# A vision tower with windowed mixer, 16-head attention and routed experts: the attention operands stacked by SBUF copies on row halves, with one reduction and one exponential per pair of heads

## What is computed

```python
q = split_heads(holo_linear(x, basis_q, phase_q, amp_q))     # 16 heads of 16
k = split_heads(holo_linear(x, basis_k, phase_k, amp_k))
attn = jnp.einsum('bhqd,bhkd->bhqk', q, k) * scale
attn = jax.nn.softmax(attn, axis=-1)
out = jnp.einsum('bhqk,bhkd->bhqd', attn, v)
```

## Time and profile before

| | |
|---|---|
| median of 3 runs | 2960.3 us (2955.33 to 2965.71) |
| the profiled execution | 2954.87 us, its span 2953.0 us |
| PE busy (matmul) over the span | 2595.7 us, 88% |
| PEld, DVE, ACT, POOL busy | 2124.6, 1788.6, 1124.9, 626.0 us |
| mean granted PE clock | 0.916 of full |
| DMA | 140.13 MB, mean 47 GB/s |

### The profile page before, as it was taken

How to read it: one execution, slowest core, us unless ns; L and a number is a source line. 1 busy time by engine, 2 the same in 40 slices (tenths; PEclk the granted TensorE clock), 3 DMA queues, 4 the chain that set the end, 5 groups by cost and what they waited for, 6 DMA issues and landing times. The chain is left out here.

```text
span 2953.0 us, 57443 instructions
## 1 busy us (share of the span) xinstructions
PE 2595.7 (88%) x16871; PEld 2124.6 (72%) x16872; DVE 1788.6 (61%) x4711; ACT 1124.9 (38%) x2993; POOL 626.0 (21%) x581
## 2 busy tenths in 40 slices
PE   2689999999999999999996557499999899999999
PEld 2467777777776776767763446377777699999999
DVE  6466767777667777767761787733333345555555
ACT  0135444445454454444452211044444423333332
POOL 1212212112122121121101675500000022222222
PEclk9589999999999999999996555599999999999999
DMA  2000000000000000000000443222222211122211
GB/s 75 8 8 23 20 16 20 23 16 20 17 23 20 16 20 19 20 20 16 16 9 14 160 131 116 93 82 83 84 85 84 78 54 57 57 64 62 59 57 54
DMA packets 88092, 140.13 MB, mean 47 GB/s; under 512 B 13986, under 2 KB 59860, under 8 KB 87764
## 3 DMA queue, kind: packets, MB, share of 16 engines
q1 hardware_dynamic: 74836, 101.99, 11.5%
q0 software_dynamic: 13056, 35.67, 3.7%
HBM read 83.04 MB, written 54.03 MB: 46 GB/s over the span
## 5 line engine op out<-in xcount | busy, mean ns | idle before, releaser
L735 DVE TENSOR_REDUCE mx<-ps 128x1 f32<-128x257 f32 x1024 | 394.5, 416 | 238.4 <-PE ps L385 214.6
L582 ACT ACTIVATE pT<-ps 128x257 f32<-128x257 f32 x1024 | 343.2, 382 | 285.1 <-PE ps L402 283.8
L385 PE MATMUL ps<-km,q 128*128 128x258 f32 x1024 | 351.3, 360 | 46.8 <-DVE mx L735 23.9
L402 PE MATMUL ps<-q,km 128*128 128x258 f32 x1024 | 283.6, 304 | 2.1 <-ACT pT L582 2.1
L385 PEld LDWEIGHTS ps<-km,q 128*128 128x128 f32 x1024 | 197.4, 193 | 118.5 <-DVE mx L735 57.2
L928 POOL TENSOR_TENSOR rs<-rs,mhalf 128x2 f32<-128x2 f32 x32 | 22.5, 703 | 1004.3 <-DVE rs L687 1004.3
L402 PEld LDWEIGHTS ps<-q,km 128*128 128x128 f32 x1024 | 192.5, 193 | 46.6 <-issue 28.7
L1564 PE MATMUL ps<-zhi,whi 128*128 128x256 f32 x1056 | 214.2, 284 | 1.5 <-DVE zlo L1632 1.5
L1564 PE MATMUL ps<-zhi,wlo 128*128 128x256 f32 x1056 | 211.1, 281 | 0.0
L1564 PE MATMUL ps<-zlo,whi 128*128 128x256 f32 x1056 | 210.6, 281 | 0.0
L1694 POOL TENSOR_TENSOR mark<-rowid 128x1 f32<-128x1 f32 x33 | 6.5, 197 | 860.4 <-DVE idx L1650 860.4
(11 more groups left out here) (321 smaller groups left out, 6278.8 us busy)
## 6 DMA issues: line engine op xcount, KB each, us to landing
z<-zs SPq DMA_DIRECT2D x140, 128.0 KB, 2.0
ys<-z SPq DMA_DIRECT2D x140, 128.0 KB, 1.9
hb<-hscr SPq DMA_DIRECT2D x66, 256.0 KB
xs<-in_x SPq DMA_DIRECT2D x64, 256.0 KB, 3.9
hscr<-h SPq DMA_DIRECT2D x34, 256.0 KB, 2.1
out<-acc SPq DMA_DIRECT2D x32, 256.0 KB
uu<-in_wu SPq DMA_DIRECT2D x6, 768.0 KB, 5.3
raw<-in_wu SPq DMA_DIRECT2D x6, 768.0 KB, 4.9
```

The source lines that it names most:

```text
L385: pe.matmul(ps[:, n % 2, 0:NP], q2[p % 2][:, h // 2, t * P:(t + 1) * P], km[p % 2][:, h // 2, h % 2, :], start=True, stop=True).then_inc(m ...
L402: pe.matmul(o, km[p % 2][:, h // 2, h % 2, t * P:(t + 1) * P], q2[p % 2][:, h // 2, :], start=True, stop=True).then_inc(s_ps, 1)
L582: act.activation(pT[:, n // LT, n % LT, :], ps[:, 4 + n % 2, 0:N], ACT.Exp, scale=HD ** -0.5).then_inc(s_ok, 1)
L735: dve.tensor_reduce(mx[:, t, h:h + 1], ps[:, n % 2, 0:N], AX_X, ALU.max, negate=True).then_inc(mx_ok, 1)
```

## The change

The selection matmuls and their copies out of PSUM go. In their place SP copies the pieces of `qhi`, `qlo`, `khi`, `klo` inside SBUF, by six DMAs for q and six for k of an image (`spread`), into `q2` and a new `k2`, of which there are now four each. In both, the even head of a pair has rows 0 to 47, the odd head rows 64 to 111, and row 48 or 112 holds the shift (in `q2`) or ones (in `k2`, written once by eight DMAs). The weights of the head projections are put into another column order to suit that.

A pair of heads is then two matmuls, one over rows 0.. and one over rows 64.., into two banks: 0 and 1 for the maxima, 4 and 5 for the scores. DVE reduces both banks with one instruction (128 x 2 x 257), ACT takes the exponential of both with one. A pair may start when the pair before it has been read out: for the maxima PE waits for reduction i-1 and both class copies, for the scores for exponential i-1.

Also: the buffers `y1` and `yT` go (the mixer writes back into `tq` and `rden`), `bdm` moves to temporary space, the input image is loaded ahead of the constants, and DVE no longer clears `qhi` to `klo`, `q2` and `km`. PE's `cls_tiles` now waits for `lo_ok` itself.

```diff
-    q2 = [sb("q2_%d" % p, [P, G2, NP], F32R) for p in range(2)]
-
-    km = [sb("km_%d" % p, [P, G2, 2, NP], F32R) for p in range(2)]
+    q2 = [sb("q2_%d" % p, [P, G2, NP], F32R) for p in range(U)]
+    k2 = [sb("k2_%d" % p, [P, G2, NP], F32R) for p in range(U)]
     bdh = sb("bdh", [P, 2, FT, P], F32R)
     bdl = sb("bdl", [P, 2, FT, P], F32R)
     negr = [sb("negr%d" % p, [P, NP], F32R) for p in range(2)]
...
-    RN = 2 * G2
-    LAG = 4
-    U = 4
+    PAIRS = LT * G2
+    MXN = PAIRS + 2
     VALUES_AT = (9, 12, 14)
 
-    MX_AT = [3, 3, 3, 2, 3, 3, 3, 2, 2, 2, 2, 2, 2, 0, 0, 0]
+    MX_AT = [2, 1, 2, 1, 1, 1, 2, 1, 1, 1, 1, 1, 1, 0, 0, 0]
     mx_upto = [sum(MX_AT[:n]) for n in range(NH + 1)]
-    assert mx_upto[NH] == SN
+    assert mx_upto[NH] == PAIRS
+
+
+    DMAS = 2 * STACKED // HD
+    PLACES = (((0, 1), (2,)), ((0, 2), (1,)))
 
 
 
...
-        for dst, src in loads:
-            sp.dma_start(dst[:], src).then_inc(c_load, 16)
         for k in range(2):
             sp.dma_start(xs[k * C:(k + 1) * C, :],
                          a["x"][0:1].rearrange("n c l h -> (n c) (l h)")).then_inc(x_in, 16)
+        for dst, src in loads:
+            sp.dma_start(dst[:], src).then_inc(c_load, 16)
         sp.wait_ge(half_ok, 1)
+        for t in k2:
+            for k in range(2):
+                row = SLOT2 * k + STACKED
+                sp.dma_start(t[row:row + 1, :, :].bitcast(F32), oner[0:24, 0:G2 * NP // 24].bitcast(F32)).then_inc(ones_in, 16)
         sp.dma_start(hscr[B], h2[:]).then_inc(h2_out, 16)
...
+
+        def spread(j, p, n):
+
+            sp.wait_ge(lo_ok, 2 * j + n + 1)
+            to, parts = (q2, k2)[n][p % U], ((qhi, qlo), (khi, klo))[n]
+            for part, places in zip(parts, PLACES[n]):
+                for place in places:
+                    for k in range(2):
+                        row = SLOT2 * k + HD * place
+                        sp.dma_start(to[row:row + HD, :, :].rearrange("d (j w) l -> d j (w l)", w=FT).bitcast(F32),
+                                     part[p % 2][SLOT2 * k:SLOT2 * (k + 1), :, :].rearrange("p w l -> p (w l)").bitcast(F32)
+                                     ).then_inc(stack_in[n], 16)
...
+            if has(b + 2):
+                spread(b + 2, p + 2, 0)
+                spread(b + 2, p + 2, 1)
...
 
-        def stack(j, p, r):
-
-            g, kind = r // 2, r % 2
-            pe.wait_ge(lo_ok, 2 * j + 1 + (r > 0))
-            if r > 0 or later(j):
-                pe.wait_ge(rep_ok, RN * j + r)
-            if r > 1 or later(j):
-                pe.wait_ge(repd_ok, G2 * j + g)
-            hi, lo = ((qhi, qlo), (khi, klo))[kind]
-            f = g // (G2 // FT)
-            pe.matmul(ps[:, 6, 0:NP], sel[:, 2 * kind, g % 4, :], hi[p % 2][:, f, :], start=True, stop=False)
-            pe.matmul(ps[:, 6, 0:NP], sel[:, 2 * kind + 1, g % 4, :], lo[p % 2][:, f, :], start=False,
-                      stop=True).then_inc(rep_ps, 1)
-
         def cls_tiles(m, p):
 
+            pe.wait_ge(lo_ok, 2 * m + 2)
             if later(m):
                 pe.wait_ge(negm_ok, m)
             for n, (hi, lo) in enumerate(((khi, klo), (qhi, qlo))):
...
-                pe.wait_ge(rep_ok, RN * m + RN - LAG)
-                pe.wait_ge(repd_ok, G2 * m + G2 - LAG // 2)
-            if n == NH - LAG:
-                pe.wait_ge(rep_ok, RN * m + RN)
-                pe.wait_ge(repd_ok, G2 * m + G2)
-            pe.wait_ge(mx_ok, m * MXN + n + 1)
-            pe.matmul(ps[:, n % 2, 0:NP], q2[p % 2][:, h // 2, t * P:(t + 1) * P], km[p % 2][:, h // 2, h % 2, :],
-                      start=True, stop=True).then_inc(mx_ps, 1)
+        def maxima(m, p, i):
+
+            t, g = i // G2, i % G2
+            if i == 0:
+                for n in range(2):
+                    pe.wait_ge(stack_in[n], 16 * DMAS * (m + 1))
+            pe.wait_ge(mx_ok, m * MXN + i + 2)
+            for k in range(2):
+                rows = slice(SLOT2 * k, SLOT2 * k + STACKED)
+                last = pe.matmul(ps[:, k, 0:NP], q2[p % U][rows, g, t * P:(t + 1) * P], k2[p % U][rows, g, :], start=True,
+                                 stop=True)
+            last.then_inc(mx_ps, 1)
 
         def turn_maxima(m):
             pe.wait_ge(mx_ok, m * MXN + MXN)
...
-
-            h, t = n // LT, n % LT
-            if n == 0:
+        def scores(b, p, i):
+
+            g, t = i // LT, i % LT
+            if i == 0:
                 pe.wait_ge(negm_in, 32 * b + 32)
-            if n >= 2 or later(b):
-                pe.wait_ge(s_ok, b * SN + n - 1)
-            o = ps[:, 4 + n % 2, 0:NP]
-            pe.matmul(o, km[p % 2][:, h // 2, h % 2, t * P:(t + 1) * P], q2[p % 2][:, h // 2, :], start=True,
-                      stop=True).then_inc(s_ps, 1)
+            if i > 0 or later(b):
+                pe.wait_ge(s_ok, b * PAIRS + i)
+            for k in range(2):
+                rows = slice(SLOT2 * k, SLOT2 * k + STACKED + 1)
+                last = pe.matmul(ps[:, 4 + k, 0:NP], k2[p % U][rows, g, t * P:(t + 1) * P], q2[p % U][rows, g, :],
+                                 start=True, stop=True)
+            last.then_inc(s_ps, 1)
 
         def values(b, p, g):
-            pe.wait_ge(s_ok, b * SN + LT * HPG * (g + 1))
+            pe.wait_ge(s_ok, b * PAIRS + LT * HPG // 2 * (g + 1))
             if g == 0:
                 if later(b):
                     pe.wait_ge(h2_ok, b)
...
-                    scores(b, p, 2 * n)
-                if len(todo) > 1:
-                    maxima(b + 1, p + 1, todo[1])
-                if has(b):
-                    scores(b, p, 2 * n + 1)
+                    scores(b, p, n)
                 if n == 1 and has(b + 2):
                     turn(b + 2)
                 if n == 2 and has(b + 2):
                     heads_qk(b + 2, 0)
-                if n < LAG and has(b + 1):
-                    stack(b + 1, p + 1, RN - LAG + n)
-                if n > LAG and has(b + 2):
-                    stack(b + 2, p + 2, n - LAG)
-                if len(todo) > 2:
-                    maxima(b + 1, p + 1, todo[2])
+                if len(todo) > 1:
...
-        def take_stack(j, p, r):
-            act.wait_ge(rep_ps, RN * j + r + 1)
-            if r % 2 == 0:
-                act.activation(q2[p % 2][:, r // 2, :], ps[:, 6, 0:NP], ACT.Copy).then_inc(rep_ok, 1)
-            else:
-                act.activation(km[p % 2][0:STACKED, r // 2, 0, :], ps[0:STACKED, 6, 0:NP], ACT.Copy).then_inc(rep_ok, 1)
+            act.activation((qhi, khi)[n][p % 2][:], ps[:, 2:4, 0:NP], ACT.Copy).then_inc(hi_ok, 1)
 
         def exps(b, n):
-            act.wait_ge(s_ps, b * SN + n + 1)
-            act.activation(pT[:, n // LT, n % LT, :], ps[:, 4 + n % 2, 0:N], ACT.Exp, scale=HD ** -0.5).then_inc(s_ok, 1)
+
+            g, t = n // LT, n % LT
+            act.wait_ge(s_ps, b * PAIRS + n + 1)
+            act.activation(pT[:, 2 * g:2 * g + 2, t, :], ps[:, 4:6, 0:N], ACT.Exp, scale=HD ** -0.5).then_inc(s_ok, 1)
 
         def take_group(b, g):
             act.wait_ge(pv_ps, b * G + g + 1)
...
-            dve.tensor_tensor(lo[p % 2][:, :, 0:N], ps[:, 2:4, 0:N], hi[p % 2][:, :, 0:N], ALU.subtract).then_inc(lo_ok, 1)
-
...
-            dve.wait_ge(mx_ps, m * MXN + n + 3)
-            t, h = n // NH, n % NH
-            dve.tensor_reduce(mx[:, t, h:h + 1], ps[:, n % 2, 0:N], AX_X, ALU.max, negate=True).then_inc(mx_ok, 1)
+        def maxima(m, i):
+            dve.wait_ge(mx_ps, m * MXN + i + 3)
+            t, g = i // G2, i % G2
+            dve.tensor_reduce(mx[:, t, 2 * g:2 * g + 2], ps[:, 0:2, 0:N], AX_X, ALU.max, negate=True).then_inc(mx_ok, 1)
 
         def cls_shift(m, p):
 
...
                         attn_stats(b + 3, p + 3)
 
 
+        dve.memset(oner[:].bitcast(F32), 1.0)
         dve.memset(h2[:], 0.0)
         dve.memset(mh65[:], -0.5)
         dve.memset(mhalf[:], -0.5).then_inc(half_ok, 1)
         dve.memset(clso[:], 0.0).then_inc(clso_ok, 1)
-        dve.memset(oner[:].bitcast(F32), 1.0)
         dve.memset(Wz[:], 0.0)
         dve.memset(one1[:], 1.0)
-        for t in (*qhi, *qlo, *khi, *klo, *q2, *km, *negr):
-            dve.memset(t[:].bitcast(F32), 0.0)
+        for t in negr:
+            dve.memset(t[0:NH, :].bitcast(F32), 0.0)
         dve.memset(mv3[:, B * LT:, :], 0.0)
         dve.memset(vbd[:], 0.0)
         dve.memset(va[0][:], 0.0)
         dve.memset(va[1][:], 0.0).then_inc(d_step, 1)
         dve.wait_ge(d_step, 1)
```

More of the change, by code:

```diff
@@ L313, in mixer_out @@
             for f in range(FT):
[L314 removed]
+                last = pe.matmul(o, rden[:, f, t * P:(t + 1) * P], outw[:, f, :], start=False, stop=(f == FT - 1),
                                  skip_group_check=True)
@@ L328, in resonances @@
             for f in range(FT):
-                last = pe.matmul(ps[0:3 * HARM, 3, 0:N], basT[:, f, :], zT[:, f, :], start=(f == 0), stop=(f == FT - 1))
```

(13 more changed lines are left out.)

71 lines of the change are left out of this document (19 added, 52 removed).

## The result

The changed kernel takes **3198.8 us** (median, 3185.8 to 3206.1) against 2957.8 us before: a ratio of **1.081 [1.0763, 1.0856]**. The forecast was 2925, its range ended at 2970, and slower had 0.14. The prediction was wrong, in sign too. In what follows medians are of all runs of a kernel, ratios and their intervals of the fast ones, which lie within 1.5% of its fastest run.

A forecast was written before the change was run, and what follows sets the result against it. TensorE looked like stage A's bound, at nearly full clock, partly tied to VectorE's reductions. Terms -17.5 - 8 + 2 - 68 + 59 = -32.5 from 2954.9 gave 2922, median 5.4 higher, forecast 2925 us, range 2845 to 2970.

The forecast's parts named there:

- The clock: Stage A's images: idle in slot 6 and from slot 15 to 0 brings 0.6 falls an image, +59 us.
- The price of a fall: Stage A: an image with a fall to 1.2 GHz takes 46.91 us instead of 43.75, so 3.2 us.
- The walk of slot 0: Slot 0 of each image: the second maxima pair costs 0.1 us.
- filling: As a forecast term, the first two images: no stacking matmuls and PSUM round trips, -8 us (0 to -15).
- The slower rival: Slots 6 and 0: clock falls more than once an image; about 3067 us at two falls; chance 0.10.
- the closed ring: Two banks written, read and rewritten in turn: a maxima pair follows the last only after 1.07 us.
- its formula: Slower rival, f falls an image: change of -23.5 + 31 x (3.2 f - 2.2) us, a loss from f = 0.93.
- The walk at full clock: Stage A's slots: -2.9 + 0.35 + 0.3 + 0.1 = -2.2 us an image, -68 over 31 images.
- Slot 6's wait: Slot 6: about 1.5 us idle before the second maxima pair; kv half 1 at about 2.1, +0.35 us.
- The new stall of 0.6 us in slot 9: Slot 9's pair waits for slot 8's reduction, late behind the reciprocals; eats slot 8's gain and costs 0.3 us.
- The start: Kernel start: VectorE takes up the constants at 14.7 instead of 32.2 us, so 17.5 us earlier.
- the rest: Draining: the last image's exponentials run in a closed ring with their pairs, +2 us (0 to +5).

The follow-up runs named there:

- e7: Changed kernel with maxima tile by tile over three banks (0, 1, 6), reductions of 257 columns; 3090.9 us, ratio to before 1.0445.
- e2: Changed kernel plus two full-height matmuls of 258 columns, read by nobody, in every slot; 3135.1 us, ratio to before 1.0589.
- e10: e6 without the five filling matmuls of slot 6; 2976.9 us, ratio to before 1.0064.
- e6: Changed kernel with layer norm z ahead of slot 0's reductions, and unread filling matmuls in slots 0, 6, 10, 15; 2930.0 us, ratio to before 0.9912.
- e1: Changed kernel plus filling matmuls, read by nobody, where TensorE idles (slots 0, 6, 10, 15); 3020.6 us, ratio to before 1.0203.
- e11: Changed kernel with three-bank maxima, z ahead of slot 0's reductions, and filling in slots 0, 6, 10, 15; 2962.4 us, ratio to before 1.0032.

## Why the prediction was wrong, by its own steps

- **The clock, the step that failed.** "I take 0.6 falls an image: +1.9 us an image, +59." The trace has about 2.5: 78 falls, and the images take 257 us more where -9 was forecast for them (-68 and +59). I weighed the places as if one idle of over a microsecond among thin matmuls were needed, and set aside the single waits of 0.5 to 0.8 us because in the kernel before they "never were" enough. There the selection matmuls stood around them; that is my reading, from e7 and e2, and not shown by itself. The wait for the mixer's product in slot 10 is the same in both kernels (the row below; 0.81 us in after), and the clock never fell behind it before, but 21 times in after; slot 0's 0.51 and 0.59 us in a row had a fall behind them too, and e10, which leaves only slot 6 unfilled, falls there in 28 of 30 images, six times ahead of the wait itself.

The kernel before, slot 10:

```profile
1031.15 0.38 PE L309 MATMUL ps<-browr,oner 64*128 64x256 f32 x1 [0.82 <-DVE yT L675]
```

- **The price of a fall** was about right: 3.2 us taken, and e10, with one an image, takes some 45.4 us instead of 42.6, 2.8 each. But falls do not only add: in after an image takes 52.8 us on average (1636.2 / 31), 10.2 above e6's, or 4.1 for each of 2.5 falls, z included. One reason is in VectorE's rows: the chain from the output product's statistics to the class copy, forecast at 8.3 us, takes 8.1 where the clock holds (8.7 before) and 11.6 to 12.2 where it has fallen in slot 10, since TensorE's part of the chain then runs at half clock.
- **z, a step that was missing.** The walk of slot 0 priced its second pair at 0.1 us and never asked what stands behind it on VectorE. Two reductions of 0.69 with an idle of 0.48 between put z behind GpSimd's split: 4.1 us for 0.73. The sign was among the rows shown: the transposes that wait 2.75 us for z, which I read as a matter of filling. With filling it is worth up to 90 us (e1 against e6, which differ in slot 0's filling as well).
- **The slower rival was right in mechanism as far as it went, and had 0.10.** It named the closed ring, slots 6 and 0, and a loss from 0.93 falls on (its formula gives 0.92). With f = 2.5 the formula gives 2960 - 23.5 + 31 x 5.8 = 3116; the other 83 us it has no term for, and z and the longer chain are two that it lacks. How they share the 83 is not shown. What I held against it, that at half clock TensorE is the bound again and brings the clock back, is true and no comfort: in after the clock is back 7 to 17 us later in most cases and falls at the next place.
- **The walk at full clock: waits too long, sum too good.** Slot 6's wait was put at about 1.5 us and is 1.10; its second pair follows the first at 1.60 us instead of 1.83, kv half 1 at 1.82 (897.67 to 899.49) instead of 2.1, where 1.75 was read before. So the prediction had this wait longer than it is and still took too few falls. The new stall of 0.6 us in slot 9 doesn't show: its pair at 852.40 has no wait. Pairs go side by side (starts 0.003 us apart); reductions 683 and exponentials 600 ns; the copies are hidden. Even so a full-clock image of 41.55 us was forecast, e6 has 42.60 with its filling, 1.15 saved instead of 2.2. How much of the gap is the filling is not known.
- **Start and ends.** The start gives 19.2 us (17.5 taken: the constants are taken up at 13.04 and not at 14.7, a time for which the prediction shows no working), filling gives +1.9 where -8 was taken, for a cause that no run followed up, and the rest +2.4 (+2).

What stays open: how much of the remaining difference between e11 and e6 is z, what the missing selection matmuls cost by themselves, and what a fall needs. The runs order the cases and give no rule.

## What to carry to other kernels

Where TensorE keeps its full clock by being nearly always busy, price a change by the idle it opens and not only by the matmuls it saves: five filling matmuls in each image's wait of 1.1 us were worth 47 us in 2977. Two banks that one wide instruction reads together are a ring of one; if a reader is widened, look for a bank or for independent matmuls to stand in the wait. And when VectorE's reductions are regrouped, list what stands behind them there and which GpSimd instruction runs then: an order that came with a gain of 90 us in one version lost 28 in another.
